# The last routed layer's results: from stores by slot with a gather at the end to a scatter per tile with plain loads

## What is computed

```
weights, idx = _gate(xf, gate_w, gate_b)                # best 2 of 16 experts, for each token
combine = (jax.nn.one_hot(idx, E) * weights[..., None]).sum(1)
h1 = jnp.einsum('td,edi->tei', xf, We1) + be1           # 16 experts, 256 -> 128
h3 = jnp.einsum('td,edi->tei', xf, We3) + be3
h = jax.nn.silu(h1) * h3
yo = jnp.einsum('tei,eid->ted', h, We2) + be2           # 128 -> 256
y = jnp.einsum('te,ted->td', combine, yo)
z = jax.nn.silu(xf @ ws1 + bs1) * (xf @ ws3 + bs3) @ ws2 + bs2
return (y + z).reshape(shape)                           # and x + that is the output
```

## Time and profile before

| | us |
|---|---|
| median of 3 runs | 1805.03 (1801.49 to 1806.5) |
| the profiled execution, its own time | 1800.73 |
| its span, first to last instruction | 1798.8 |
| PE / DVE / ACT / POOL busy | 1549.0 / 1130.6 / 765.1 / 562.0 |

### The profile page before, as it was taken

The page is one execution under the profiler, slowest core; times in us unless marked ns, Lnnn a source line. Parts: engine busy times, 40 slices in busy tenths (PEclk is TensorE's granted clock), DMA queues, the critical chain, the costliest instruction groups (busy, mean ns, idle before and its releaser), DMA issues.

```text
span 1798.8 us, 33124 instructions
## 1 busy us (share of the span) xinstructions
PE 1549.0 (86%) x10736; PEld 1151.7 (64%) x10736; DVE 1130.6 (63%) x2842; ACT 765.1 (43%) x1659; POOL 562.0 (31%) x766
## 2 busy tenths in 40 slices
PE   5999958979999999977989999389999999777970
PEld 4665626966666666656879999356566666665850
DVE  5888874347778888876621212467787777675423
ACT  3555556435545555545212222045555555432420
POOL 3111124034444111120023333167752110425526
PEclk9999968989999999977999999699999999686995
DMA  4000000010000000010068989400000000013984
GB/s 175 2 0 0 1 24 24 1 36 10 12 9 7 1 1 0 0 59 24 36 233 321 327 320 330 147 1 1 0 10 13 9 12 6 11 55 95 377 219 138
DMA packets 46682, 137.01 MB, mean 76 GB/s; under 512 B 6445, under 2 KB 29118, under 8 KB 40448
## 3 DMA queue, kind: packets, MB, share of 16 engines
q1 hardware_dynamic: 32288, 110.05, 17.4%
q0 software_dynamic: 7536, 19.67, 3.5%
q10 hardware_dynamic: 6768, 6.16, 1.0%
HBM read 119.21 MB, written 17.56 MB: 76 GB/s over the span
## 4 chain that ended last, share of the span: by engine, by line
PE 55%; DVE 20%; issue 8%; DMA 6%; ACT 4%; POOL 4%; DVEq 1%; POOLq 0%; SPq 0%; ACTq 0%
PE ps L779 9%; PE ps L959 8%; PE ps L826 7%; PE ps L1078 7%; PE ps L859 4%; DVE negmax L1474 4%; PE ps L874 4%; PE ps L1090 4%; PE ps L838 3%; DMA row_in<-rows_of,from_u 3%; PE ps L851 3%; DVE probs_all L1482 2%; PE ps L777 2%; DMA back_of<-w_odd 2%; POOL y_back L630 1%
## 5 line engine op out<-in xcount | busy, mean ns | idle before, releaser
L779 PE MATMUL ps<-km,qk 128*128 128x512 f32 x640 | 321.0, 600 | 4.6 <-ACT km L1143 4.6
L1149 ACT ACTIVATE probs_all<-probs_all 128x512 f32<-128x512 f32 x256 | 161.3, 630 | 186.6 <-DVE probs_all L1482 186.5
L1474 DVE TENSOR_REDUCE negmax<-ps 128x4 f32<-128x512 f32 x256 | 174.6, 682 | 47.9 <-PE ps L779 46.5
L1078 PE MATMUL ps<-hT,w_tile 128*128 128x128 f32 x1624 | 200.3, 279 | 3.6 <-DMA w_tile<-in_w_f 2.9
L638 POOL TENSOR_SCALAR eps_sum<-mv 128x1 f32<-128x1 f32 x112 | 25.4, 226 | 564.8 <-DVE mv L1414 526.7
L1078 PEld LDWEIGHTS ps<-hT,w_tile 128*128 128x128 f32 x1624 | 191.8, 195 | 5.4 <-DMA w_tile<-in_w_f 3.4
L1482 DVE TENSOR_TENSOR probs_all<-ps,negmax 128x512 f32<-128x512 f32 x256 | 177.1, 692 | 19.2 <-DVE negmax L1474 1.5
L859 PE MATMUL ps<-const,probs_all 128*128 128x128 f32 x1024 | 160.8, 280 | 12.6 <-ACT probs_all L1149 12.3
L779 PEld LDWEIGHTS ps<-km,qk 128*128 128x128 f32 x640 | 118.4, 193 | 76.7 <-issue 64.1
L1142 ACT ACTIVATE probsT_all<-ps 128x512 f32<-128x512 f32 x256 | 148.1, 592 | 7.5 <-PE ps L859 7.3
L1520 DVE TENSOR_SCALAR km<-qk,const 128x256 f32<-128x256 f32 x512 | 139.8, 348 | 4.6 <-ACT qk L1143 2.6
(11 more groups left out here) (241 smaller groups left out, 3113.8 us busy)
## 6 DMA issues: line engine op xcount, KB each, us to landing
w_tile<-in_w_f SPq DMA_DIRECT2D x39, 1536.0 KB
w_tile<-in_w_f SPq DMA_DIRECT2D x47, 385.0 KB, 6.2
back_of<-w_odd ACTq DMA_DIRECT2D x47, 128.0 KB, 6.0
ctxT<-in_ctxT SPq DMA_DIRECT2D x32, 128.0 KB, 2.1
rows_of<-row_of SPq DMA_DIRECT2D x8, 512.0 KB, 3.8
y_back<-back_of SPq DMA_DIRECT2D x8, 512.0 KB, 4.8
w_even<-in_w_att SPq DMA_DIRECT2D x3, 1024.0 KB, 5.9
w_raw<-in_w_f SPq DMA_DIRECT2D x2, 1026.0 KB, 5.5
```

The costliest lines, as they stand in the source:

```text
L779: mm(ps[:, g, :], qk[:, p, stationary + c, :], km[:, c, j:j + HB, :].rearrange("p h k -> p (h k)"), start=mask is None, stop=True).then_in ...
L1078: last = mm(ps[:, 2 * which + at.two, fc * P:(fc + 1) * P], w[:, col:col + P], rowT[:, at.two, c, :], start=c == 0, stop=c == KC - 1)
L1149: nc.scalar.activation(probs[:, g], probs[:, g], ACT.Exp, scale=HD ** -0.5).then_inc(S["probs"], 1)
L1474: nc.vector.tensor_reduce(m, bank, AX.X, ALU.max, negate=True).then_inc(S["dve_sm"], 1)
```

## The change

In `MOE1` results now take the way that they take in `MOE0`. ScalarE's 47 stores, GpSimd's 32 gathers and their semaphores go. VectorE works out `to_u` for `MOE1` as well (three small operations more). GpSimd's queue gets a `send_back` for each of the 47 tiles, and SyncE's queue gets the 8 plain loads behind the last weight load and ahead of the output stores. `back_dram` of `MOE1` has 4,096 rows in place of 6,016. VectorE's copy of result j waits for the scatter of tile j-4 where it waited for its store.

```diff
@@ load_results, on SyncE
                 for b in range(BUFS):
-                    sp.wait_ge(S["y_out%d" % b], 16 * rounds(f, F_TILES[f], b))
+                    sp.wait_ge(S["y_out%d" % b], 16 * uses_before(f, F_TILES[f], b))
+                if f == MOE1:
+                    sp.wait_ge(S["bias_done"], NT // 2)
@@ SyncE's program
             load_tiles(MOE1)
+            load_results(MOE1)
@@ move_rows, on GpSimd
                     if j + BUFS < n:
                         fetch(f, j + BUFS)
-                    if f == MOE0:
-                        send_back(f, j)
-
-            def fetch_results():
...
-                for t in range(NT):
-                    if t >= 2 * GT:
-                        pool.wait_ge(S["combined"], NT + t - 2 * GT + 1)
-                    for k in range(2):
-                        nc.gpsimd.indirect_dma_start(y_back[:, t // GT % 2, k, t % GT], None, back_dram[MOE1],
...
+                    send_back(f, j)
@@ ScalarE
-            def store_result(f, j):
-
-                b = j % BUFS
-                act.wait_ge(S["t_y"], tiles_before(f, j + 1))
-                act.dma_start(back_dram[f][j * P:(j + 1) * P], y_sb[:, b]).then_inc(S["y_put%d" % b], 16)
@@ slots, step 5, on VectorE
+                    ts(from_u[:, 0:m], b, -1.0, 0.0, ALU.add, ALU.max).then_inc(S["from_sb"], 1)
+                    link(ts(c, nth_, 0.0, NOWHERE, ALU.is_equal, ALU.mult))
+                    link(stt(out=a, in0=grp_, scalar=float(P), in1=nth_, op0=ALU.mult, op1=ALU.add))
+                    dve.wait_ge(S["from_sb"], f - MLP)
+                    stt(out=to_u[:, 0:m], in0=a, scalar=-1.0, in1=c, op0=ALU.add, op1=ALU.add).then_inc(S["from_done"], 1)
@@ tiles, on VectorE
                 if rounds(f, j, b):
-                    dve.wait_ge(S[("y_out%d" if f == MOE0 else "y_put%d") % b], 16 * rounds(f, j, b))
+                    dve.wait_ge(S["y_out%d" % b], 16 * uses_before(f, j, b))
...
-                    if f == MOE1:
-                        dve.wait_ge(S["got%d" % (t % (2 * GT))], 32 * (t // (2 * GT) + 1))
-                    elif t % GT == 0:
-                        dve.wait_ge(S["back_in%d" % (g % 2)], 32 * (g // 2 + 1))
+                    if t % GT == 0:
+                        dve.wait_ge(S["back_in%d" % (g % 2)], 64 * ROUTED.index(f) + 32 * (g // 2 + 1))
```

More of the change, by code:

```diff
@@ L232, in build @@
         from_u = sb("from_u", [P, F_TILES[MOE1]], u32)
-        to_u = sb("to_u", [P, F_TILES[MOE0]], u32)
+        to_u = sb("to_u", [P, F_TILES[MOE1]], u32)
         steps_of = sb("steps_of", [P, 16])
@@ L308, in build @@
                      "n_sq n_var n_rstd n_norm n_base n_out n_sb fT_hi_sb fT_sb lg_out lg_sb dve_n pool_n "
-                     "x_in0 x_in1 x_in2 x_in3 const_in rows_in late_in tokens_sb rows_out scan scan_done rank_out rank_sb slots_sb experts_sb part_sb row_hot tile_hot tile_nth tile_grp hot_out from_sb from_done row_in0 row_in1 row_in2 row_in3 w_tile_in0 w_tile_in1 w_tile_in2 w_tile_in3 w_tile_in4 w_tile_in5 w_tile_in6 w_tile_in7 be2_in weights_sb comb2_sb comb_sb combT_out combT_sb bias_out bias_sb bias_done row_out rowT_sb t_gate t_up t_act t_h t_down t_y y_out0 y_out1 y_out2 y_out3 y_put0 y_put1 y_put2 y_put3 back_in0 back_in1 got0 got1 got2 got3 got4 got5 got6 got7 combined  w_att0 w_att1 w_att2 w_att3 w_att4 w_raw_in f_bias_sb w_hi_sb w_lo_sb setup passed gate gate_p "
+                     "x_in0 x_in1 x_in2 x_in3 const_in rows_in late_in tokens_sb rows_out scan scan_done rank_out rank_sb slots_sb experts_sb part_sb row_hot tile_hot tile_nth tile_grp hot_out from_sb from_done row_in0 row_in1 row_in2 row_in3 w_tile_in0 w_tile_in1 w_tile_in2 w_tile_in3 w_tile_in4 w_tile_in5 w_tile_in6 w_tile_in7 be2_in weights_sb comb2_sb comb_sb combT_out combT_sb bias_out bias_sb bias_done row_out rowT_sb t_gate t_up t_act t_h t_down t_y y_out0 y_out1 y_out2 y_out3 back_in0 back_in1 combined  w_att0 w_att1 w_att2 w_att3 w_att4 w_raw_in f_bias_sb w_hi_sb w_lo_sb setup passed gate gate_p "
                      "gate_out up_out act_done h_done hi_done hid_done down_out acc_done act_gate stored").split():
@@ L402, in build @@
         rows_dram = {f: nc.dram_tensor("rows_of_%d" % f, (NT * P, D), f32, kind="Internal").ap() for f in ROUTED}
-        back_dram = {f: nc.dram_tensor("back_of_%d" % f, (2 * NT * P if f == MOE0 else F_TILES[f] * P, D), f32, kind="Internal").ap() for f in ROUTED}
+        back_dram = {f: nc.dram_tensor("back_of_%d" % f, (2 * NT * P, D), f32, kind="Internal").ap() for f in ROUTED}
         def before(f):
@@ L496, in load_results @@
                     if g >= 2:
-                        sp.wait_ge(S["combined"], (g - 1) * GT)
+                        sp.wait_ge(S["combined"], NT * ROUTED.index(f) + (g - 1) * GT)
                     for k in range(2):
@@ L617, in move_rows @@
                         fetch(f, j + BUFS)
-                    if f == MOE0:
-                        send_back(f, j)
-            def fetch_results():
-                for b in range(BUFS):
-                    pool.wait_ge(S["y_put%d" % b], 16 * rounds(MOE1, F_TILES[MOE1], b))
-                pool.wait_ge(S["bias_done"], NT // 2)
-                for t in range(NT):
-                    if t >= 2 * GT:
-                        pool.wait_ge(S["combined"], NT + t - 2 * GT + 1)
-                    for k in range(2):
-                        nc.gpsimd.indirect_dma_start(y_back[:, t // GT % 2, k, t % GT], None, back_dram[MOE1],
-                                                     bass.IndirectOffsetOnAxis(ap=slot_u[:, k, t:t + 1], axis=0)
-                                                     ).then_inc(S["got%d" % (t % (2 * GT))], 16)
+                    send_back(f, j)
             def inverse_root(tile, which, p):
@@ L754, in _ @@
             move_rows(MOE1)
-            fetch_results()
         @block.tensor
@@ L1385, in tiles @@
                     tile_gate(f, j)
-                    if f == MOE1 and j >= 3:
-                        store_result(f, j - 3)
-                if f == MOE1:
-                    for j in range(n - 3, n):
-                        store_result(f, j)
             act.wait_ge(S["const_in"], 32)
```

## The result

The changed kernel takes **1911.96 us** (median of 4 runs, 1906.83 to 1917.88), the kernel before 1804.05 (1801.49 to 1806.5): a ratio of 1.0599 [1.0564, 1.0634]. It is 108 us slower, where 97 were forecast and 1902 us. The profiled execution has a span of 1909.1 us, 110.3 over the 1798.8 of before.

What follows compares the result with a forecast made beforehand. A GpSimd fetch-scatter loop with TensorE was to bound the tile stage: 1669.7 + 191.7 + 5.3 + 29.0 gives a 1895.7 us span, 97 over before, hence 1902 us against the median; range 1866 to 1948.

Steps and rivals of the forecast that it cites:

- The loop: Last layer's tile stage: fetch j+5 queues behind scatter j, which awaits its copy; 9.35 us per two steps, 4.675 a tile.
- w: TensorE's step in the tile stage, first turn to end of down product: 2.33 us, bounds 1.86 and 2.80.
- copy to scatter: Tile stage, from the end of VectorE's copy to the start of GpSimd's scatter: 0.81 us.
- scatter to fetch: GpSimd's queue in the tile stage, scatter start to start of the fetch behind it: 1.32 us.
- F: Tile stage, a row fetch from issue to landing: 3.9 us, bounds 2.8 and 5.6.
- The start: Start of the last layer's tile stage: `to_u` costs 0.5 us before the first fetch; step 4 starts at 1669.7.
- The last tile and the end: Turning tile 46 to its last copy takes 5.3 us; loads, sums and output store after it take 29.0.
- Nothing else moved: Tile stage: scatter buffers freed over 15 us later, weight loads eight tiles ahead, ScalarE's dropped issues: all costed at nothing.
- Not slower: Rival, chance 0.06: tile stage keeps its pace, shorter end decides, 1785 us; no slower below 2.31 us a tile.
- A crowded DMA: Rival, chance 0.18: slow DMA throughout the tile stage, fetches landing in 5.6 us, low clock; 1948 us.
- VectorE holds GpSimd off: Rival, chance 0.06: GpSimd's indirect issues wait while VectorE works, up to 0.8 us a tile, 33 us; 1935 us.
- The queue's rate: Rival, chance 0.08: GpSimd's issue binds the tile stage at 2.6 us a tile; 1817 us.

Runs made afterwards that it cites:

- wait_alone: Kernel before plus only a wait in GpSimd's queue for VectorE's copy of result j ahead of fetch j+5, stores and gathers kept: 1890.28 us.
- late_scatter: Changed kernel with each last-layer scatter placed three tiles later in GpSimd's queue: 1807.82 us, and 1834.32 us on another chip.
- lag_one: Changed kernel with TensorE's lag in the last layer 1 instead of 2, result j made in step j+1: 1834.84 us.
- filler: Changed kernel with six unread TensorE products behind each last-layer tile's down product: 1889.59 us.

## Why the prediction was right, step by step

Direction, mechanism and size held: a span of 1895.7 us was forecast and 1909.1 measured. The 13.4 us between lie here.

- **The loop** was the right one, and `wait_alone` and `late_scatter` show its cause, with `lag_one` beside them: the wait's place in the queue. Its terms in the round above, with the forecast in brackets: w 3.26 us (2.33), VectorE 0.81 (0.89), copy to scatter 0.81 (0.81), scatter to fetch 1.32 (1.32), F 3.77 (3.9), landing to TensorE 0.12 (0.1), together 10.1 (9.35). Over the 41 steps it took 4.87 us a tile, not 4.675: 199.7 us for 191.7, so +8.0.
- **The term that was mis-sized is w.** The prediction took "the middle, 2.33, with bounds 1.86 and 2.80". In that round it was 3.26, above the upper bound. The bound came from a step that was only partly at half clock. The earlier trace rows has its turn's weight load still at 0.20 us, while here it takes 0.29; and its eight up products, the first line here, took 1.67 us where the round above has 1.92, the second line (timelines of before and of after):

```profile
1721.78 1.67 PE L1078 MATMUL ps<-hT,w_tile 128*128 128x128 f32 x8
```

```profile
1722.49 1.92 PE L1066 MATMUL ps<-hT,w_tile 128*128 128x128 f32 x8
```

The clock was granted at 0.70 on average, inside the 0.6 to 0.9 that was forecast, but I should have taken w at half clock for the whole step. By itself this error is worth (3.26 - 2.33) / 2 x 41 = 19 us, and only +8.0 came out: the VectorE and fetch terms of the round are 0.2 us shorter than forecast, and not every round was as long as the one shown (9.74 us on average; those that began at 1748.10 and 1756.27 took 8.2 and 8.9). That the loop came so close is in part luck.
- **F** was close: on the chain that ended last, the fetch that opens a pair took 2.6 to 4.4 us with a median of 3.7, against 3.9; the sampled landings of all fetches have a median of 2.8. On the Trainium skill's page "DMA: Bandwidth & Descriptors", section "Anatomy of one DMA — SWDGE (gpsimd) path", the estimate was 2.3 us. No sampled landing was under 2.6, so the measured rows were the better source.
- **The start** was 1.9 us late: the first turn after fetch 5 came at 1671.59 and not 1669.7. The first fetch went out 3.4 us later than before, of which 1.34 was GpSimd's wait for `to_u` (0.5 taken) and about 2 were there already in the layer before: its last stage of TensorE starts at 1613.19, where it did at 1611.10. A faster landing, 3.4 us for 3.9, gave some back.
- **The last tile and the end.** From the turn of tile 46 to its copy's end took 6.9 us and not 5.3, at half clock again. The end took 1909.1 - 1878.19 = 30.9 us and not 29.0: its last scatter starts 2.1 us after the copy and not 0.8, since the last scatters queue up at 1.3 us each, which `MOE0` at lag 1 did not show. The loads up to the last sum took 23.3 us where `MOE0`'s took 21.9, and what follows the last store's start took 0.8 less than before; the output stores, costed at nothing, run beside these loads, but whether they slow them was not tried. That is +1.6 and +1.9.
- **Nothing else moved**, as costed: scatters landed in 2.1 to 4.1 us against over 15 allowed, and the waits list none of VectorE for a scatter and 0.3 us in all for a buffer of rows.
- **Rivals.** "Not slower" fell with the loop in the trace, and its point of decision, 2.31 us a tile, is also why `late_scatter` with 2.61 gains nothing. "A crowded DMA" fell: the share was 0.38 to 0.45 and F at most 4.4, with a median of 3.7, and not 5.6. "VectorE holds GpSimd off" fell: the 47 fetch issues took 0.946 to 1.108 us with a median of 0.975, so 0.03 more than in the earlier trace rows and not 0.4. The prediction set a rule of the Trainium skill beside this rival ("SBUF — State Buffer", section "SBUF: two separate sides"). Its example of a copy in a two-port mode is one of fp32 from SBUF to SBUF, while VectorE's copy and `h_in` here read PSUM (`w_odd<-ps`, `h_in<-ps,w_tile,act_sb`), so nothing in this stage tests the rule. "The queue's rate" was wrong for the change and right for `late_scatter`: 1817 worked out, 1807.82 measured, and 1834.32 on the other chip.

## What to carry to other kernels

In a DMA queue that is worked in order, ask of every wait which prefetch stands behind it: one wait on the newest result turned fetches that ran four tiles ahead into a loop of two tiles. The same scatter placed three tiles later left the kernel 0.3% slower than before on one chip and 1.7% on another, instead of 6%. Work out the issuing engine's own pace too, since a scatter and a fetch by GpSimd cost 2.6 us a tile together, more than the 2.31 at which the shorter end would have paid. Give padding entries of an indirect transfer addresses of their own, or none.

## What the runs showed that was not expected

- Indirect fetches of which many descriptors read one row of DRAM took the transfer rate down to 220 GB/s with the DMA engines 0.97 busy; spread over 128 rows, 331 GB/s at 0.90, and 9.6 us off the kernel.
- TensorE, which worked in bursts of two steps with holes of some 4 us between them, had a granted clock of 0.70; six useless products a tile brought it to 0.97 and the kernel from 1911.96 to 1889.59 us, although TensorE's own work, useless products included, then set the pace.
- One program, `late_scatter`, took 1807.82 us on one chip and 1834.32 on another, while the kernel before kept to 1803 on both. The cause is open.
- The layer's first fetch, which nothing ahead of the layer should move, started at 1651.5 us before, at 1652.7 in `late_scatter`, 1654.9 in the changed kernel, 1656.3 in `filler`, 1656.8 in `wait_alone` and 1661.3 in `lag_one`. `to_u` is only 1.3 us of that. A profiled execution therefore carries some microseconds from elsewhere, and a stage is best compared from its own first fetch; why they differ was not looked into.
